# Macaron block with two mixtures of experts: the second routing made inside attention, queries stacked by DMAs

## The reference

```
x = x + 0.5 * moe(layernorm(x))      # 8 experts, top 2 by softmax(x @ gate_w),
                                     # each gelu(x @ fc_w[e]) @ proj_w[e], 128 -> 512 -> 128
x = x + attention(layernorm(x))      # 16 query heads of 64, one shared key and value head,
                                     # bias by relative position, causal softmax, @ Wout + bout
x = x + 0.5 * moe(layernorm(x))      # the same weights as the first
```

## Time and profile before

| | |
|---|---|
| median of 3 runs | 1218.73 us (1217.48 to 1219.61) |
| the profiled execution: its time, its span | 1218.79 us, 1217.1 us |
| busy share PE, PEld, DVE, ACT, POOL | 80%, 67%, 61%, 53%, 52% |
| first mixture: loop over 72 tiles | about 104 to 244 us |
| attention | about 245 to 923 us |
| second routing | about 923 to 999 us |
| second mixture: loop over 72 tiles | about 999 to 1185 us |
| answers read back, added, written out | about 1185 to 1217 us |

### The profile page before, as it was taken

How to read it: one execution, slowest core, us unless ns; L and a number is a source line. 1 busy time by engine, 2 the same in 40 slices (tenths; PEclk the granted TensorE clock), 3 DMA queues, 4 the chain that set the end, 5 groups by cost and what they waited for, 6 DMA issues and landing times.

```text
span 1217.1 us, 23933 instructions
## 1 busy us (share of the span) xinstructions
PE 977.7 (80%) x7212; PEld 821.4 (67%) x7212; DVE 748.1 (61%) x2441; ACT 639.3 (53%) x1671; POOL 627.0 (52%) x457
## 2 busy tenths in 40 slices
PE   1516999918888999999999999999996238888870
PEld 1516999916666777777777777877775237777760
DVE  4682222249898888888788888786874662222226
ACT  1201333318778888888888888887873002222220
POOL 2144444367777444535445454454541147777773
PEclk9996999958999999999999999999997569999995
DMA  6888788710010000000000000000002025555546
GB/s 194 129 98 267 209 208 209 178 47 25 25 27 23 1 2 2 1 2 1 1 2 2 1 2 2 2 1 2 1 2 70 0 58 153 152 153 154 148 105 207
DMA packets 66825, 87.14 MB, mean 72 GB/s; under 512 B 8802, under 2 KB 38500, under 8 KB 66704
## 3 DMA queue, kind: packets, MB, share of 16 engines
q1 hardware_dynamic: 57344, 66.60, 20.2%
q0 software_dynamic: 9360, 19.03, 7.2%
HBM read 65.15 MB, written 20.97 MB: 71 GB/s over the span
## 4 chain that ended last, share of the span: by engine, by line
PE 65%; DVE 12%; DMA 9%; issue 5%; POOL 4%; ACT 3%; another core or an unknown queue 0%; DVEq 0%; SPq 0%; POOLq 0%; ACTq 0%
PE bank L1171 12%; PE bank L1155 11%; PE bank L1148 8%; PE bank L1098 7%; PE bank L1108 7%; PE bank L1149 6%; DMA xr<-xn_dram,gidx 5%; PE bank L1178 5%; DVE in_tile L856 2%; PE bank L1055 2%; PE bank L1034 2%; POOL y_dram L587 2%; PE bank L1035 1%; PE bank L1036 1%; PE bank L1090 1%
## 5 line engine op out<-in xcount | busy, mean ns | idle before, releaser
L633 POOL TENSOR_TENSOR prob<-prob,rsum 128x512 f32<-128x512 f32 (+3 forms) x128 | 296.0, 2321 | 267.4 <-DVE rsum L999 267.3
L701 ACT ACTIVATE prob<-prob,negmax 128x384 f32<-128x384 f32 (+3 forms) x512 | 282.9, 554 | 57.2 <-DVE negmax L992 53.9
L992 DVE CUSTOM_DVE_ANT_0 prob<-bank,bias_tab 128x384 f32<-128x384 f32 (+3 forms) x512 | 237.6, 486 | 68.0 <-PE bank L1149 61.3
L675 ACT ACTIVATE hT<-bank 128x512 f32<-128x512 f32 x144 | 86.0, 597 | 328.2 <-PE bank L1098 328.2
L1148 PE MATMUL bank<-kst,qst 128*128 128x256 f32 (+2 forms) x512 | 192.2, 385 | 12.9 <-DVE negmax L992 10.0
L581 POOL DMA_INDIRECT xr<-xn_dram,gidx x144 | 138.0, 958 | 118.6 <-PE bank L1090 67.9
L1155 PE MATMUL bank<-ident,prob 128*128 128x128 f32 x1280 | 190.0, 275 | 0.0
L924 DVE COPY yo<-bank 128x128 f32<-128x128 f32 x144 | 42.1, 292 | 210.7 <-PE bank L1108 195.0
L1171 PE MATMUL bank<-pT,vst 128*64 128x256 f32 x1280 | 166.4, 389 | 4.9 <-DVE pT L1005 3.1
L1155 PEld LDWEIGHTS bank<-ident,prob 128*128 128x128 f32 x1280 | 152.4, 141 | 25.6 <-issue 11.4
L1149 PE MATMUL bank<-kst,qst 128*128 128x256 f32 (+2 forms) x512 | 162.9, 327 | 0.0
(11 more groups left out here) (153 smaller groups left out, 1252.6 us busy)
## 6 DMA issues: line engine op xcount, KB each, us to landing
w1t<-L_ffn_fc_w SPq DMA_DIRECT2D x144, 256.0 KB
bias_dram<-hg SPq DMA_DIRECT2D x1, 5120.0 KB, 52.9
y_dram<-yo SPq DMA_DIRECT2D x72, 64.0 KB
xn_dram<-in_tile SPq DMA_DIRECT2D x8, 512.0 KB, 3.0
bias_tab<-bias_dram SPq DMA_DIRECT2D x1, 4096.0 KB, 13.1
in_tile<-y_dram SPq DMA_DIRECT2D x8, 512.0 KB, 4.4
xr<-xn_dram,gidx POOLq DMA_INDIRECT x144
x_sb<-L_attn_x SPq DMA_DIRECT2D x4, 512.0 KB, 9.3
```

The lines of the kernel that those rows point to most:

```text
L633: g.tensor_tensor(out=pv, in0=pv, in1=rsum[:, n % 8, :].unsqueeze(2).to_broadcast([P, HG, (n % QT + 1) * P]), op=ALU.mult).then_inc(norm_d ...
L701: a.activation(prob[n % 8][:, h, :], prob[n % 8][:, h, :], ACT.Exp, scale=-1.0, bias=negmax[:, i % 8:i % 8 + 1], accum_out=lsum[:, n % 8, ...
L992: v.tensor_tensor_reduce(out=prob[n % 8][:, h, :], in0=BANK_OF["S", b, n, h][:, 0:w], in1=bias_tab[:, HG * (n // QT) + h, SEQ - w:SEQ], sc ...
```

## The change

Four things change together.

1. **Second routing as tasks.** The 32 tiles are cut in groups of 8, 8, 8, 4, 2 and 2. As soon as attention has finished the rows of a group, planner tasks do its share of the routing: V2, A2, I2 the deviation, X2 the normalised rows (into `slot`), T2, C2, L2, G2 transposes and router product, H2 the two choices, W2 and W3 the weights, P2 and B2 the prefix sum, with a running count `run` carried from group to group.
2. **Rows scattered to slots.** The list is not turned round any more. Each expert owns 4096 rows of `slot_dram`; SC (POOL) scatters every normalised row, with its number and first choice in two more columns, to the next free slot of both its experts (2 indirect DMAs of 128 rows x 130 numbers for each tile). Slots that no row takes have to say so: 17 DMAs of about 1 MB, issued by ACT behind every second O task of the first 33 units, fill `slot_dram` with a number out of range. `second_lists` only makes the list of tiles (`etile`, `rowi`) after attention.
3. **Second loop.** `xr` of a tile is now one block of `slot_dram`, loaded by SP with a row number read from `rowi`. POOL only scatters the answers. DVE makes `sidx` of each tile from the two columns, one instruction of 128x1.
4. **Queries.** QH and QL work on all 128 partitions at once, into `qhl` (one buffer), and SP moves the four quarters to `qst` by 4 DMAs of 128 KB within SBUF. The scores wait for these (`q_in`), and so does the next QH. The planner's costs for QH and QL go from 0.98 and 1.1 to 0.5 and 0.62, with 3.0 for the landing. `yg`, the buffer of GA, shares memory with `slot` and has one set in place of two, so GA of a sequence waits for CB of the one before.

```diff
+                for q in range(QT):
+                    task(("ST", b * QT + q), {"dve": 0.25}, [("YA", b, NU - QT + q)])
+            for i, group in enumerate(GROUPS):
+                task(("V2", i), {"dve": 1.7}, [("ST", t) for t in group])
+                task(("A2", i), {"act": 3.4}, [("V2", i)])
...
+                    task(("SC", t), {"pool": 2.6}, [("B2", i, 1)])
+                    task(("T2", m), {"pe": 0.5}, [("X2", t) for t in PIECES[m]], "front")
...
+                task(("P2", i), {"pe": 0.3}, [("H2", i, 1)], "front")
+                task(("B2", i, 0), {"dve": 1.5}, [("P2", i)], None, ("P2", i))
+                task(("B2", i, 1), {"dve": 1.2}, [("B2", i, 0)])
...
+                        sp.reg_load(slot_row, rowi[0:1, n:n + 1])
+                        row = sp.snap(slot_row, min_val=0, max_val=E * ROWS)
+                        if n >= 4:
+                            sp.wait_ge(sidx_done, n - 3)
+                        sp.dma_start(xr[:, n % 4, :], slot_dram[ds(row, P), :]).then_inc(xr_in[n % 4], 16)
...
+            def restack_sp():
+                for i, k in enumerate(RESTACKED):
+                    sp.wait_ge(misc_free, MISC_FREE[k])
...
+                    for o in range(2):
+                        for z in range(2):
+                            sp.dma_start(qst[z * DH:(z + 1) * DH, g % 2, 2 * c + o, :].bitcast(F32), qhl[o * DH:(o + 1) * DH, z, :].bitcast(F32)).then_inc(q_in, 16)
...
-                        for o in range(2):
-                            a.activation(qst[0:DH, g % 2, 2 * c + o, :], BANK_OF["Q", b, g, c][DH * o:DH * o + DH, :], ACT.Copy,
-                                         scale=DH ** -0.5).then_inc(misc_hi, 1)
+                        if Q_IN["QL", b, g, c] > 64:
+                            act.wait_ge(q_in, Q_IN["QL", b, g, c] - 64)
+                        a.activation(qhl[:, 0, :], BANK_OF["Q", b, g, c][:], ACT.Copy, scale=DH ** -0.5).then_inc(misc_hi, 1)
...
+                        if (b * NU + n) % 2 == 0 and b * NU + n < 2 * FILLS:
+                            fill_act((b * NU + n) // 2)
...
+                            v.scalar_tensor_tensor(out=sidx[:, n:n + 1], in0=xr[:, n % 4, D + 1:W], scalar=rvt[:, n:n + 1],
+                                                   in1=xr[:, n % 4, D:D + 1], op0=ALU.not_equal, op1=ALU.add).then_inc(sidx_done, 1)
```

More of the change, by code:

```diff
@@ L24 @@
 EPS = 1e-5
+ROWS = TILES * P
+W = D + 2
+NOWHERE = 1.0e5
+GROUPS = [range(0, 8), range(8, 16), range(16, 24), range(24, 28), range(28, 30), range(30, 32)]
+PIECES = [range(t, min(t + QT, group[-1] + 1)) for group in GROUPS for t in group[::QT]]
+FILLS = 17
 MASKED = -3.0e38
@@ L105, in build @@
         pos_row = sb("pos_row", [P, PAIRS], I32)
+        fill = sb("fill", [P, W])
+        id_row = sb("id_row", [P, TILES])
+        first_row = sb("first_row", [P, E])
+        run = sb("run", [P, E])
         base = nc.sbuf_base
@@ L319, in wanted_at @@
             at = b * PERIOD
+            if kind in ("V2", "A2", "I2", "H2", "W2", "W3", "P2", "B2"):
+                return pre_at(GROUPS[b], kind) + (task[2] if kind in ("H2", "B2") else 0)
+            if kind in ("T2", "C2", "L2", "G2"):
+                group = [group for group in GROUPS if PIECES[b][0] in group][0]
+                return pre_at(group, kind) - (group[-1] - PIECES[b][-1])
+            if kind in ("ST", "X2", "SC"):
+                group = [group for group in GROUPS if b in group][0]
+                return pre_at(group, kind) - (group[-1] - b)
             if kind in ("S", "TTR", "EXP", "R", "N"):
@@ L383, in attention_order @@
                         for other in known[user]:
-                            hop = HOP["landing" if k[0] == "GA" else "same" if other == e else "pe" if e == "pe" else "other"]
+                            hop = HOP["landing" if k[0] in ("GA", "QL") else "same" if other == e else "pe" if e == "pe" else "other"]
                             known[user][other] = max(known[user][other], busy[e] + hop)
@@ L412, in build, with group_of, half, slots_of @@
         XA_DONE, PROJ_DONE = counted("dve", ("LN",), QT), counted("dve", ("YA",))
+        RESTACKED = [k for k in ORDER["dve"] if k[0] == "QL"]
+        Q_IN = {k: 64 * (i + 1) for i, k in enumerate(RESTACKED)}
         NORM, BOUT = counted("pool", ("N",)), counted("pool", ("BO",))
         YG_DONE = counted("dve", ("CB",), 2)
+        XN2_DONE = counted("dve", ("X2",))
+        XNT2_PS, XNT2_SB, LOGIT2_PS, LOGIT2_SB = counted("pe", ("T2",)), counted("act", ("C2",)), counted("pe", ("L2",)), counted("dve", ("G2",))
+        def group_of(t):
+            return [t in group for group in GROUPS].index(True)
+        def half(t):
+            return t // QT % 2
+        def slots_of(tiles):
+            return slice(tiles[0] % (2 * QT), tiles[-1] % (2 * QT) + 1)
         PLACE = {k: i for e in ORDER for i, k in enumerate(ORDER[e])}
@@ L442, in build @@
                     in_order(("S", b2, g2 * QT + QT - 1, h), k)
+        for first, second in zip(RESTACKED, RESTACKED[1:]):
+            in_order(("QH", *first[1:]), ("QH", *second[1:]))
         for k in ORDER["dve"]:
@@ L890, in ffn_dve @@
             def ffn_dve(r):
-                everything = slice(0, TILES)
                 if r == 0:
+                    everything = slice(0, TILES)
                     for i in range(4):
@@ L1119, in attention_pe @@
                             pe.wait_ge(*freed(TAKEN_FROM[k]))
-                    if kind == "xT":
+                    if kind == "T2":
+                        pe.wait_ge(xn2_done, max(XN2_DONE["X2", t] for t in PIECES[b]))
+                        for q, t in enumerate(PIECES[b]):
+                            ins = t_.transpose(out[:, q * P:(q + 1) * P], slot[:, t % (2 * QT), 0:D], ident[:])
+                        ins.then_inc(xnT2_ps, 1)
+                    elif kind == "L2":
+                        pe.wait_ge(xnT2_sb, XNT2_SB["C2", b])
+                        for q in range(len(PIECES[b])):
+                            ins = t_.matmul(out[:, q * E:(q + 1) * E], xnT2[:, q * P:(q + 1) * P], gate_sb[:], start=True, stop=True)
+                        ins.then_inc(logit2_ps, 1)
+                    elif kind == "P2":
+                        nt = len(GROUPS[b])
+                        pe.wait_ge(hot2_done, b + 1)
+                        hot = hot2b[:, slots_of(GROUPS[b]), :].rearrange("p t e -> p (t e)")
+                        t_.matmul(out[:, 0:nt * E], ones_bf[:], hot, start=True, stop=True)
+                        t_.matmul(out[:, 2 * QT * E:(2 * QT + nt) * E], before[:], hot, start=True, stop=True).then_inc(prefix2_ps, 1)
+                    elif kind == "xT":
                         pe.wait_ge(xa_done, XA_DONE["LN", b])
```

414 lines of the change are left out of this document (309 added, 105 removed).

## The result

The changed kernel takes 1267.35 us (median of 4 runs, 1263.34 to 1270.38), the kernel before on the same chip 1218.11. The ratio is 1.0402, with an interval of 1.0368 to 1.0435: slower by 49 us, where I forecast 56 us faster. Two later measurements on other chips gave 1.0385 and 1.0392.

The account below looks back on a forecast made before the run. It held PE to bound the first loop and attention, POOL's issuing the second loop, with a routing hole between: 1218.8 - 46 - 42 + 12 + 12 + 4 + 10 - 6 = 1163 us, range 1122 to 1205.

Parts of the forecast that it names:

- Routing between attention and loop, -46: From attention's last output add to the second loop's first matmul: 30.6 us in place of 76.4, bounds -54 to -31.
- Second loop, -42: Second loop runs at PE's pace instead of POOL's issuing: -45, less 3 us for late fetches; bounds -45 and -20.
- Stacking by DMAs, +12 and +4: Attention: queries land 3.6 us after QL, mostly covered, +12 (bounds +4, +85); first scores wait one landing longer, +4.
- the landing sets attention's pace: Rival, attention: landing over 5 us stalls PE, 86 us in place of 12; 1237 to 1267 us; 5 in 100.
- PE's work for the groups, +12 (6 to 18): Attention: transposes, router passes, prefix products and hops for 28 of 32 tiles add 12 us on PE; bounds +6, +18.
- Fills, +10 (2 to 40): Attention: the 17 fills take ACT's time and their bytes stand beside the queries' DMAs; +10 us, bounds +2 and +40.
- the collision: Rival, first two sequences of attention: fills cost ACT 34 us and queries' landing is 6 us; 1198 us; 10 in 100.
- Relief of DVE and ACT, -6: Attention: DVE and ACT time saved per chunk, mostly given back by the groups' DVE steps; -6 us, bounds -25 and 0.
- a sequence over 4 us longer in the middle of attention: Sign, attention: the forecast is wrong if a mid-attention sequence takes more than 4 us longer than before.

Follow-up runs that it names:

- e6: Changed kernel with two buffers for the halves of the queries, one per chunk with its own semaphore, in place of one; 1251.37 us, ratio 1.0265, chip A.
- e7: Changed kernel with the plan told 4.5 us in place of 3.0 for the queries' landing, same instructions in another order; 1224.93 us, ratio 1.0069, chip A.
- e9: Changed kernel with queries written straight to their place as before (no DMAs within SBUF) and 6 fills in place of 17; 1184.18 us, ratio 0.9727, chip A.
- e17: The changed kernel run once more, nothing altered; 1265.63 us, ratio 1.0392 to the kernel before, chip A.
- e18: Changed kernel with 1536 slots for each expert in place of 4096, so 6 fills in place of 17; 1232.1 us, ratio 1.0116, chip A.
- e15: Changed kernel with old queries and 6 fills, POOL's product of a unit issued as four, one per head; 1202.31 us, ratio 0.9455, chip B.
- e3: Changed kernel with queries written straight to their place as before and 6 fills in place of 17; 1215.6 us, ratio 0.9567, chip B.
- e8: Changed kernel with old queries, 6 fills and scatters of different tiles at least 5 us apart in the plan; 1181.75 us, ratio 0.9703, chip A.
- e4: Kernel before with only the queries' stacking by DMAs and its plan costs added; old routing and loop, no fills; ratio 1.0437 (+54 us), chip B.
- e12: Kernel before with only the queries' stacking by DMAs added, run again on chip A; 1278.05 us, ratio 1.0479 (+60 us).
- e13: Changed kernel with old queries and 6 fills, plus ten more one-input reductions of the logits on DVE in each group; 1229.93 us, ratio 0.9674, chip B.

## Why the prediction was wrong

- *Routing between attention and loop, -46: right.* -47. The list was ready at 1084.3, 23 us after the last add (25.4 forecast); the last scatter left POOL at 1083.6.
- *Second loop, -42: right.* -45, the full bound. The fetch is never late but at the start (PE waits 15 us for it in all). The loop moves 198 GB/s at a DMA share of 0.68, against 145 and 0.51 before, so it was issue time that had set its pace, as I had argued.
- *Stacking by DMAs, +12 and +4: this step failed.* It cost 54 to 60 us alone, and with the small fill in the changed kernel 48 on chip A (1232.1 - 1184.2) and 31 on chip B (1246.8 - 1215.6); why less there is not shown. The rival "the landing sets attention's pace" was the right one, but I let it decide only from 5.0 us. The landing was 4.2, and I said that each half us beyond 3.6 costs 22: that is 12 + 26. The 26 are an issue of the wrong size: I took 0.33 us, that of `w1t`, and they take 0.60; the 0.7 of the earlier trace rows, which I kept for the upper bound, was nearer. The missing rest, some 20 us, has other sources. I held PE's work between product and scores against the landing, from an order that the planner had made for 3.0 us, and counted ACT's standing still at nothing. ACT lost 60 us, and what it does not do PE lacks later. e6 and e7 bear on both: 15 us for ACT's wait, 42 for the order. And I left out the clock. These are the stretches of attention, before, e9 and after, with the columns of the earlier trace rows:

```profile
244.00:922.00 678.00, 630.54 (x4443) 489.73 (x4442) 540.55 (x1829) 532.10 (x1495) 367.37 (x200) 0.97 0.03 8
244.00:973.00 729.00, 648.03 (x4532) 498.29 (x4533) 616.89 (x2027) 559.47 (x1544) 422.30 (x256) 0.97 0.10 21
245.00:1061.00 816.00, 673.82 (x4532) 518.66 (x4532) 558.37 (x1957) 523.30 (x1483) 422.98 (x256) 0.93 0.34 73
```

  e9 and after have the same number of matmuls, yet PE is busy 25.8 us longer in the latter, at a granted clock of 0.93 against 0.97. Of the 87 us between them, 61 are PE standing still and 26 the same matmuls running slower.
- That this rival's sum, 1267 us, is the measured time is luck: it was made of a landing of 5.3 us and fills at 40 us, and had nothing of what the groups cost.
- *PE's work for the groups, +12 (6 to 18): within its bounds.* PE's busy time in attention is 630.5 us before and 648.0 in e9, 17.5 more at the same clock.
- *Fills, +10 (2 to 40): within its bounds, for the wrong reason.* Not ACT's issues (6 us in all) but the queries' landing of up to 8 us: 33.5 us beside the stacking, 1 to 3 without (on chip B). I named the collision as a rival of its own, on top of a stacking that was itself small. The two do not simply add up; my reading is that the stacking had already used up the cover that a landing has.
- *Relief of DVE and ACT, -6: this step failed too.* With the stacking gone and the small fill (e9) attention is 51 us longer. With the old queries DVE saves nothing, so PE's +12 would be all of it; the groups' steps, which I only let give back what DVE saves, had no price of their own. They have one, as 52 us of hold-ups by POOL's products come on top of their plain time (about 45 in the changed kernel). The trace had shown it, in a row from which I took one number only: in the earlier trace rows DVE's one-hot of 4096 elements takes 8.27 us beside POOL's products. The next of the same shape, after POOL's second product has ended at 982.69, takes 4.41. The timeline of the kernel before has both of POOL's products apart, and in early attention a step of 0.34 us, the adding of an answer, that ends with a product of the probabilities:

```profile
968.22 6.29 POOL L570 TENSOR_TENSOR which<-which,tile_val 128x2304 bf16<-128x2304 bf16 x1 [45.21 <-DVE which L852]
974.47 8.22 POOL L570 TENSOR_TENSOR which<-which,tile_val 128x2304 bf16<-128x2304 bf16 x1
983.23 4.41 DVE L856 TENSOR_TENSOR in_tile<-iota_p,posf 128x4096 bf16<-128x4096 f32 x1
...
294.84 3.60 POOL L633 TENSOR_TENSOR prob<-prob,rsum 128x2048 f32<-128x2048 f32 x1 [1.58 <-DVE rsum L999]
295.28 3.30 DVE L949 SCALAR_TENSOR_TENSOR x_sb<-yg,gw,x_sb 128x128 f32<-128x128 f32 x1
```

  The large ones take turns: POOL's first product ends at 974.51, DVE's one-hot 4.28 us later at 978.79, POOL's second product 3.9 us after that, though their rows overlap. So POOL waits for DVE as well. That POOL was "half idle" I read as room; the other half was a lock on DVE.
- *The sum by parts.* Attention: 51 (groups) + 48 (stacking) + 34 (fills beside it) = 133 of the 139 us; the rest is within what these runs differ by. These are steps of one path, from e17 by e18 and e9 to the kernel before, so they add up by construction; another order would share them out otherwise. From the last matmul of the loop to the end it takes 36.2 us in place of 32.5, a term that I did not have: 1218.8 - 47 - 45 + 139 + 4 = 1270, against 1268.6 for the profiled execution.
- What I named as a sign of a wrong forecast, a sequence over 4 us longer in the middle of attention, is what came: from the start of one sequence to the next it took 86 to 103 us from the third to the seventh, in place of 77 to 79.

What stays open: how the groups' 51 us divide between hold-ups, the 7 us of PE's and 10 of DVE's plain work in each group of eight, and the two table loads of 1.28 us that each group puts on ACT. In e15 13 us of time go with 12.5 us of hold-ups; as sequences without a group changed too, that the two are equal proves nothing. A version without any hold-up was not run. Nor was e15 run on chip A.

**The best version** is e15: old queries, small fill, products in four, 0.9455 [0.9433, 0.9477] to the kernel before on chip B. Part of that is the chip: e3 has 0.9567 there and the same kernel 0.9727 on chip A. On chip A the best one run is e8, 1181.75 us, 0.9703 [0.967, 0.9736].

## What to carry to other kernels

A DMA put between a product and its user inside a pipelined stage costs the whole series of issues and the landing, and a planner that is told too short a time for it loses more than the DMA itself: measure it in a small run first, write it into the plan, then judge. Two costs that share one cover are not to be added up one by one. And before small steps with two inputs in SBUF are moved to VectorE beside a busy GpSimd, look at how long one product of GpSimd is, for that is what each of them can wait; if it must be there, try the product in pieces.

## What the runs showed of the hardware

- The same kernel takes 1218 us on one chip and 1272 on another. The kernel before was traced on chip A alone, but e4 and e12 have its second loop, and there most of the difference lies: 186 us in e12 and 226 in e4, on chip B, whose row is

```profile
1064.00:1290.00 226.00, 173.79 (x1220) 164.02 (x1220) 34.85 (x142) 42.66 (x72) 137.06 (x138) 0.87 0.41 119
```

  at a clock of 0.87. Attention takes about 742 us in both. The changed second loop takes 139 to 144 us on either sort, so on chip B the change gains 84 us there and not 45. Why that loop is slower on chip B is not shown.
- Between e9 and e3 (one kernel, chips A and B) sequences without a group take 79 and 87 us, those with a group of eight 94.6 and 95 to 96. In one without a group the clock is 1.00 and 0.96, and PE is busy 76.9 and 80.2 us; that is 3 of the 8 us, and the rest is PE standing still, which was not traced to a cause.
- Four DMAs of 128 KB within SBUF, from one queue: 0.60 us for each issue and 1.8 us from the last issue to the landing at best, 5.5 us in the chunk shown beside the writing of the fills.
- The issue of a fill of 975 KB on ACT's queue takes 0.38 us, less than that of 128 KB within SBUF.
- While a DVE step with two inputs in SBUF stands for POOL's product, a reduction beside the same sort of product runs in 0.22 us or less (e13).
